# A five-step gated graph network: x and the bias row loaded ahead of the last step's operands, gate r's seeds and the weights' sums at other places in the queues of DVE and ACT

## What is computed

```python
for _ in range(5):
    s_in = state @ in_W.T + in_b
    s_out = state @ out_W.T + out_b
    a = concatenate([A @ s_in, A.T @ s_out, state])
    r = sigmoid(a @ r_W.T + r_b)
    z = sigmoid(a @ z_W.T + z_b)
    joined = concatenate([A @ s_in, A.T @ s_out, r * state])
    h_hat = tanh(joined @ h_W.T + h_b)
    state = (1.0 - z) * state + z * h_hat
out = tanh(state @ o1_W.T + o1_b) @ o2_W.T + o2_b
return layernorm(x + out)
```

## Time and profile before

| | |
|---|---|
| median of 3 runs | 1040.41 us (1038.47 to 1041.48) |
| profiled execution | 1037.02 us |
| its span, first to last instruction | 1035.2 us |
| PE busy | 993.9 us, 96% |
| DVE, ACT, POOL busy | 666.0, 425.4, 35.3 us |
| granted TensorE clock, mean | 0.987 |

### The profile page before, as it was taken

One profiled execution on the slowest core, in us unless ns is written; L12 is line 12 of the kernel. 1 busy time (PEld: TensorE's weight loads), 2 busy tenths in 40 slices (PEclk: granted clock), 3 DMA queues, 4 the chain that ended last, 5 costly groups with the idle time before them and its releaser, 6 DMA issues.

```text
span 1035.2 us, 11766 instructions
## 1 busy us (share of the span) xinstructions
PE 993.9 (96%) x4576; PEld 450.9 (44%) x4576; DVE 666.0 (64%) x1052; ACT 425.4 (41%) x594; POOL 35.3 (3%) x43
## 2 busy tenths in 40 slices
PE   7999999998999999999999999999999999977995
PEld 3444444443444444444444444444444444433443
DVE  5999968995884348467634765763367477516756
ACT  3666565541453226334412643341255245302443
POOL 0311000000000000000000000000000000002100
PEclk9999999998999999999999999999999999998998
DMA  9999991334610543462045247402534650141101
GB/s 345 386 396 407 379 290 31 77 82 117 183 41 2 161 123 72 92 183 82 1 122 148 62 72 188 123 1 82 158 70 84 155 163 2 41 148 41 41 1 41
DMA packets 199110, 134.32 MB, mean 130 GB/s; under 512 B 61712, under 2 KB 191376, under 8 KB 194960
## 3 DMA queue, kind: packets, MB, share of 16 engines
q1 hardware_dynamic: 196752, 125.20, 41.6%
q0 software_dynamic: 2304, 8.39, 2.1%
HBM read 102.11 MB, written 16.78 MB: 115 GB/s over the span
## 4 chain that ended last, share of the span: by engine, by line
PE 79%; DVE 12%; ACT 3%; issue 3%; DMA 2%; SPq 1%; POOL 0%; ACTq 0%; DVEq 0%; POOLq 0%
PE bank L1499 31%; PE bank L1597 24%; PE bank L1610 10%; PE bank L1625 6%; PE bank L1441 5%; DMA areg<-in_x 2%; ACT areg L636 1%; PE bank L1687 1%; PE bank L1668 1%; DVE scal L829 1%; DVE xop_words L806 1%; DVE w L839 1%; DVE pq_words L963 0%; DMA xop_words<-pq_words 0%; DVE areg L1215 0%
## 5 line engine op out<-in xcount | busy, mean ns | idle before, releaser
L1499 PE MATMUL bank<-areg,xop_words 128*128 128x512 fp8e4 x1792 | 395.2, 382 | 18.4 <-DVE pq_words L1188 13.3
L1499 PEld LDWEIGHTS bank<-areg,xop_words 128*128 128x128 f16 x1792 | 175.2, 98 | 236.0 <-DVE pq_words L1188 15.8
L636 ACT ACTIVATE areg<-pq_words 128x512 f16<-128x512 f32 x72 | 45.4, 630 | 237.0 <-DVE pq_words L1181 118.4
L1597 PE MATMUL bank<-areg,w 128*128 128x512 f16 x576 | 131.0, 379 | 0.0
L1441 PE MATMUL bank<-areg,xop_words 128*128 128x512 fp8e4 x512 | 112.3, 379 | 3.5 <-ACT areg L484 3.2
L540 ACT ACTIVATE tmp<-bank,bias_sb,scal 128x512 f32<-128x512 f32 x72 | 55.8, 775 | 104.1 <-PE bank L1597 104.1
L1597 PEld LDWEIGHTS bank<-areg,w 128*128 128x128 f16 x576 | 56.4, 98 | 68.0 <-DVE areg L1215 0.2
L1441 PEld LDWEIGHTS bank<-areg,xop_words 128*128 128x128 f16 x512 | 49.4, 98 | 65.8 <-issue 7.4
L484 ACT ACTIVATE areg<-tmp 128x2048 fp8e4<-128x2048 int32 x32 | 61.1, 1910 | 39.9 <-DMA tmp<-in_adj_t 21.0
L1597 PE MATMUL bank<-split,w 128*128 128x512 f16 x288 | 70.0, 379 | 2.4 <-issue 1.9
L1215 DVE SCALAR_TENSOR_TENSOR areg<-pq_words,areg 128x512 f16<-128x512 f32 x72 | 49.8, 692 | 32.7 <-ACT areg L636 31.9
(11 more groups left out here) (178 smaller groups left out, 1007.8 us busy)
## 6 DMA issues: line engine op xcount, KB each, us to landing
areg<-kept_operands SPq DMA_DIRECT2D x112, 512.0 KB, 4.3
tmp<-in_adj SPq DMA_DIRECT2D x16, 1024.0 KB, 7.2
tmp<-in_adj_t SPq DMA_DIRECT2D x16, 1024.0 KB, 8.0
kept_operands<-xop_words POOLq DMA_DIRECT2D x11, 512.0 KB, 8.2
areg<-in_x SPq DMA_DIRECT2D x8, 512.0 KB, 6.9
kept_operands<-areg SPq DMA_DIRECT2D x4, 1024.0 KB, 9.7
kept_operands<-tmp POOLq DMA_DIRECT2D x5, 512.0 KB, 3.3
pq_words<-in_gate_w SPq DMA_DIRECT2D x6, 384.0 KB, 5.4
```

Source lines behind the costliest of these rows:

```text
L636: nc.scalar.activation(y_dst(g, name)[:, 0, :], src, ACT.Copy, scale=PSC).then_inc(s_yh, 1)
L1499: last = nc.tensor.matmul(dst[:, :], xop[:, m // 2, operand_block(xo, part, m % 2), :], place8[:, mo, m, :], start=first and m == pairs[0] ...
L1597: last = nc.tensor.matmul(dst[:, :], w16[:, k, wp, feat(gi)], rhs, start=False, stop=i == KT - 1 and (wp, xp) == PASSES[-1], skip_group_ch ...
```

## The change

On SP the bias row and x's first two column blocks are issued at the start of the last step, ahead of the operand loads of its groups 1 to 3. On ACT and DVE gate r's seeds stand ahead of group 0 instead of within group 1. In step 1 `weight_hi(0)` stands behind `copy_p1` of group 0, `weight_lo(0)` behind `sums_v` of group 0, and `weight_hi(1)` one block earlier. In group 0 of every step `sums_u` stands ahead of y11's low half, and y21's sum ahead of t2's.

```diff
--- before.py
+++ after.py
@@ -407,7 +407,17 @@
                 sp.wait_ge(s_kept_a[i], 16 * len(range(i, RING_A, 3)))
             for i in range(2):
                 sp.wait_ge(s_kept_b[i], 16 * len(range(i, GATE_JOBS, 2)))
+            def load_rest(c):
+                if c >= 2:
+                    sp.wait_ge(s_out[c % 2], 32)
+                sp.dma_start(y[:, c % 2, :, :], x_v[:, c * JC:(c + 1) * JC, :]).then_inc(s_xr[c % 2], 16)
+
             for t in range(1, STEPS):
+                if t == LAST:
+                    sp.wait_ge(s_xl, 2 * CH * LAST)
+                    sp.dma_start(b2_all, o2_b.partition_broadcast(P)).then_inc(s_b2, 16)
+                    load_rest(0)
+                    load_rest(1)
                 for at in range(4 * (t - 1) + 1, 4 * t + 1):
                     if at < 4 * LAST:
                         load_group(at)
@@ -415,14 +425,10 @@
                     for c in range(CH):
                         turn_rows(CH * t + c)
 
-            sp.wait_ge(s_xl, 2 * CH * LAST)
-            sp.dma_start(b2_all, o2_b.partition_broadcast(P)).then_inc(s_b2, 16)
-            for c in range(CH):
-                if c >= 2:
-                    sp.wait_ge(s_out[c % 2], 32)
-                sp.dma_start(y[:, c % 2, :, :], x_v[:, c * JC:(c + 1) * JC, :]).then_inc(s_xr[c % 2], 16)
-                if c in (1, 2):
-                    store_rows(sp, c - 1)
+            store_rows(sp, 0)
+            load_rest(2)
+            store_rows(sp, 1)
+            load_rest(3)
             store_rows(sp, CH - 2)
             store_rows(sp, CH - 1)
             sp.wait_ge(s_out[0], 16 * CH)
@@ -641,16 +647,15 @@
 
             def group(t, g):
                 copy_p1(t, g)
-                if g == 1:
-                    for i in range(4):
-                        pair_seed(t, 0, i)
+                if t == 1 and g == 0:
+                    weight_hi(0)
                 if t == LAST and g >= 2:
                     head_act(g - 2)
                 if g == 3:
                     for gi in range(2):
                         seed(CH * t + 2, 2, gi)
                 for name in Y_ORDER[g]:
-                    if t == 1 and g == 1 and name == "y11":
+                    if t == 1 and g == 1 and name == "t3":
                         weight_hi(1)
                     y_hi(t, g, name)
                     if g == 1 and name == "y21":
@@ -749,8 +754,8 @@
             for t in range(1, STEPS):
                 n = CH * t - 1
                 rows_hi(n, 1)
-                if t == 1:
-                    weight_hi(0)
+                for i in range(4):
+                    pair_seed(t, 0, i)
                 group(t, 0)
                 split_hi(0, split_at(t, 0), CH * (t - 1) + 2)
                 split_hi(1, split_at(t, 1), CH * (t - 1) + 2)
@@ -1250,9 +1255,9 @@
 
             def group(t, g):
                 at = 4 * (t - 1) + g
+                sums_u(t, g)
                 if g == 0:
                     y_lo(t, g, "y11")
-                sums_u(t, g)
                 if t == 1 and g == 1:
                     weight_full(1)
                 if t == LAST and g >= 2:
@@ -1263,9 +1268,8 @@
                 sums_v(at)
                 if t == 1 and g == 1:
                     weight_sums(1)
-                if g == 1:
-                    for i in range(4):
-                        pair_degree(t, 0, i)
+                if t == 1 and g == 0:
+                    weight_lo(0)
                 y_sum(t, g, "y22")
                 y_lo(t, g, "y22")
                 y_sum(t, g, "y12")
@@ -1275,6 +1279,7 @@
                         y_sum(t, g, "t3")
                         y_lo(t, g, "t1")
                         y_lo(t, g, "t3")
+                        y_sum(t, g, "y21")
                     else:
                         y_sum(t, g, "t3")
                         y_lo(t, g, "t3")
@@ -1285,7 +1290,8 @@
                         y_lo(t, g, "t1")
                     y_sum(t, g, "t2")
                     y_lo(t, g, "t2")
-                    y_sum(t, g, "y21")
+                    if g == 1:
+                        y_sum(t, g, "y21")
                     y_sum(t, g, "t4")
                     y_lo(t, g, "y21")
                     y_lo(t, g, "t4")
@@ -1394,7 +1400,8 @@
                     degree_differences()
                     weight_full(0)
                     weight_sums(0)
-                    weight_lo(0)
+                for i in range(4):
+                    pair_degree(t, 0, i)
                 group(t, 0)
                 split_lo(0, split_at(t, 0))
                 split_lo(1, split_at(t, 1))
```

## The result

| | before | after |
|---|---|---|
| median of 4 runs | 1039.44 us | 1013.52 us (1012.65 to 1014.76) |
| profiled execution | 1037.02 us | 1013.64 us |
| its span | 1035.2 us | 1011.9 us |
| PE busy | 993.9 us | 989.0 us |
| PE idle in its span | 41.3 us | 22.9 us |

A forecast was written before the change was run, and what follows sets the result against it. The prediction took PE's work plus its idle time as the bound. Its terms summed to 22.6 us, less 0.2 for POOL and 0.1 rounding: 22.3 off the 1040.41 median gave 1018.1 us, range 1012.5 to 1022.5.

The forecast's parts named there:

- D: Step 1, behind PE's wait for ACT's copy: the clock no longer falls for the 24 matmuls there, 2.7 us gained.
- B: Last step, group 2, behind the wait for y21's sum: PE's clock no longer falls, 1.7 us gained.
- A: Last step, group 2: early x and bias row remove PE's wait for y21's sum, 11.1 us gained.
- C: Step 1: seeds and then ACT's copy ahead of weight_hi(0) cut PE's wait for sum_1 from 3.86 to 1.15, 2.7 us gained.
- Rival 1: Step 1: the clock still falls after a wait of 1.15 us; gain 19.6, time 1020.8 us; chance 0.16.
- E: Group 0, four steps: sums_u ahead of y11's low half removes PE's waits for sums_u, 1.0 us gained.
- F: Group 0: y21's sum ahead of t2 removes PE's remaining small waits for that sum, 2.2 us gained.
- G: Step 1, group 1: without the degree rows PE's 1.31 us wait for t2's low half goes, 1.2 us gained.
- Rival 2: DVE held back by POOL at last step's start, or late in step 1 after weight_lo(0); time near 1022 us; chance 0.07.
- Rival 4: Last step, group 1: PE waits for operand loads queued behind x, kernel slower; time 1044 us; chance 0.02.
- rival 3: Last step, group 3: another wait replaces the 11 us one; gain 16.8 if half returned, time 1023.6 us; chance 0.04.
- rival 5: No change: residual(0) held by something else despite early x, step 1 gains taken back; time 1040 us; chance 0.01.

The follow-up runs named there:

- x alone: Kernel before with only the SP part: bias row and two x loads issued at the last step's start; 0.9875 of before, median 1024.93 us.
- x late: Changed kernel with the SP part undone, x and bias row behind all operand loads again; 0.9911 of before, median 1028.41 us.
- seeds and weights alone: Kernel before with only the moved seeds, degree rows and weight sums of ACT and DVE; 0.9941 of before, median 1031.62 us.
- x behind group 2: Changed kernel with bias row and two x loads issued behind the operand loads of the last step's group 2; 0.9771 of before, median 1013.78 us.
- the kernel with the copy first: Changed kernel with ACT's four seeds behind the copy into sum_1 in step 1 only; 0.9755 of before, median 1012.41 us.

## Why the prediction was right, point by point

The way and the place of each gain were as forecast, but for 0.35 us in step 2. The size of the small waits and the step from the profile to the median were off, and the size of D was one draw of a range. The time, 1013.5 us, lies in the range, 4.6 us under the forecast 1018.1. It lies below the 1015 to 1021 that the prediction gave its likeliest case; only the allowance downward, for the gap between profile and median, takes it in.

Every gain below is a difference of two profiles, and that of before is the one from which the prediction took its prices. So a full agreement shows that the wait went away, and says little on how well a price holds in other executions. The other profiles tell that for B and D.

- **A and B, x early** (11.1 + 1.7): 12.94 us in the stretch, of which 11.08 are the wait, 1.7 the slow matmuls and the rest the restart. x alone shows that it stands by itself, and x late in the changed kernel that it comes back in full. The two margins held: 1.8 us for y21's sum, and no wait in group 3. The load was faster than forecast: 5.9 us from the bias row's issue to POOL's start (801.20 to 807.07), where the prediction took 7.4 from the row of before. B was 1.7 in the profiled execution, and 1.4 to 2.3 in other profiles with this wait (16 matmuls in 5.06 to 5.93 us).
- **C, the copy** (2.7): 3.86 to 1.23 us, 2.6.
- **D, the clock behind it** (2.7): 2.7 in the comparison of the two profiles (24 matmuls in 8.04 us before), but 1.6 to 1.7 in three other profiles. The step that the clock does not fall after 1.15 us was right, in all profiles with 1.2 us and even with 2.46. That the sum came out right here is luck: the size was that of one execution, and another profile of before could have had 1 us less. Rival 1 fell.
- **E and F, DVE's order** (1.0 + 2.2): 3.40 us in steps 2 to 4 and 1.0 in step 1, together 4.4. The step that failed is the term's unit: I took the idle times for the cost of a wait, and each of the 8 restarts costs a little more. In steps 2 to 4 the idle times before add up to 2.66 us and the stretches shrank by 3.40. The prediction also expected nothing in steps 2 to 4 from moving the seeds and degree rows, and seeds and weights alone took 0.35 us off the wait for y21's sum in step 2; the sum was not hurt by it, because DVE's order removes that wait whole.
- **G, the first gate** (1.2): 1.53, the whole wait of 1.31 and 0.2 with its restart. The low half was in time with `weight_hi(1)` ahead of t3.
- **POOL beside DVE** (-0.2): nothing. The additions fell at 807.07 to 812.58, in which DVE's rows on the critical path read a bank and one SBUF operand and took 0.68 to 0.69 us as ever. The sum t1, for which the prediction feared, ran only at 814.10, 1.5 us behind the last addition, so the forecast meeting with it did not take place. The rule of the Trainium skill (SBUF — State Buffer, "SBUF: two separate sides") names two SBUF inputs of VectorE. By it these rows are not held up, and the trace agrees. The meeting with column block 2's additions is still there (4 of them in 4.20 us), hidden as before. My warning that each of 8 additions might cost DVE one took the rule too widely. Rival 2 fell, its second half by the 0.26 us that `weight_lo(0)` had to spare.
- **Loads behind x** (nothing): no view of any kernel names an operand load as what PE waited for in steps 1 to 4. Rival 4 fell with it, rival 3 because group 3 of the last step has no wait, and rival 5 by the result. Two profiles (x alone, x behind group 2) have a pause of PE of 0.25 and 0.24 us in step 3, ahead of any load of x, for which the views name nothing.
- **From the profile to the median**: I subtracted 22.3 us from 1040.41, the median of three runs, and kept the 3.4 us between it and the profiled execution. That gap belonged to those three runs and not to the kernel: the medians of before in two later comparisons were 1037.31 and 1038.12, and the changed kernel's profiled execution lies 0.1 us from its median. Forecast against its own profile, 1014.7, the miss is 1.1 us: the stretches gained 1.6 us more than the 22.3 of the sum, and the changed kernel reached step 1 0.6 us later. Of the rest of the 4.6, 3.4 come from that step.

## What to carry to other kernels

A large idle time of the busiest engine can be a late DMA issue seen through several engines, as it was here. Follow the releasers back until one of them waited for nothing but its place in a queue, count the time from that issue to the restart (14 us here, with load, additions and sums), and issue the transfer that much ahead; here more lead bought nothing, and one place less cost 7.6 us. When small waits are priced from a profile, add the restart to each, and price the low clock behind a long one as a range. Where the profiled execution and a median of three runs differ by more than the smallest term, forecast from the profiled execution.

## What the runs showed of the hardware

- In steps 1 to 4, between dense matmuls, the granted clock stayed at 1.00 behind PE's idle times of 1.2, 1.3 and 2.46 us, as it did behind one of 1.9 us in step 0, and fell to 0.50 behind those of 3.00, 3.86, 4.55 and 11 us. The windows behind 2.46 and behind 3.00 us (stretch: us, busy us, matmuls, granted clock, DMA):

```profile
245.14:251.00 5.86, 5.86 (x27) 1.00 0.31 87
```

```profile
246.50:248.50 2.00, 2.00 (x6) 0.50 0.07 21
```

- This is no sharp bound. After 3.33 us, at the end of each kernel and with the same work ahead, it differed from one execution to the next: the 24 matmuls of 256 columns behind it took 2.79 us in the kernel with the copy first, and 4.17 to 5.30 in the 13 other profiles:

```profile
999.24 5.30 PE L1694 MATMUL bank<-o,pq_words 128*128 128x256 f16 x24 [3.33 <-DVE areg L1115]
```

- Near 21 us in step 0 PE waits in every kernel, 2.84 to 4.49 us in these profiles. The clock fell behind 2.84, 3.12, 3.15, 3.30 and 3.40 us and stayed at 1.00 behind 3.23, 3.31 and 3.61. The changed kernel did both: the clock fell behind 3.73 us in its first profile, and not behind 3.61 us in its second. The windows of the two:

```profile
23.00:25.00 2.00, 2.00 (x7) 0.50 1.00 414
```

```profile
21.00:27.00 6.00, 6.00 (x28) 1.00 0.97 375
```

- How long it stays low differs too: behind the same 3.86 us wait 1.6, 1.6, 1.7 and 2.7 us were lost, behind the same 11 us wait 1.4, 1.7, 2.1 and 2.3. The Trainium skill (TensorE: Matmul & The Clock Gate, Part 1) says, of a kernel's start, that the number of slow matmuls varies from run to run of one kernel. These traces show the same behind waits in the middle, in kernels that are alike there. The prediction still said that no row showed it, and took both losses from one profile.
